# The silu of z as one ScalarE function, two channel blocks to a table load, in place of a tanh and a VectorE product, with small stages moved around it

## The reference, cut to what matters

```python
xz = xn @ W_in
xb, z = jnp.split(xz, 2, axis=-1)
xb = conv_w[:, 0] * xp[:, :-2] + conv_w[:, 1] * xp[:, 1:-1] + conv_w[:, 2] * xp[:, 2:] + conv_b
xb = jax.nn.silu(xb)
dt = jax.nn.softplus(xb @ W_dt + b_dt)
...                      # scan over time: h = exp(dt*A)*h + dt*x*B ; y = sum over states of h*C
y = (y + D_param * xb) * jax.nn.silu(z)
return residual + y @ W_out
```

## Time and profile before

| | |
|---|---|
| median of 3 runs | 2643.23 us (2642.23 to 2643.57) |
| the profiled execution's own time | 2637.64 us |
| its span, first to last instruction | 2635.9 us |
| mean granted TensorE clock | 0.949 |
| busy share PE, DVE, POOL, ACT | 87%, 91%, 86%, 56% |
| slot 6, first to next first scan | 153.8 us |

### The profile page before, as it was taken

The page is one execution under the profiler, slowest core; times in us unless marked ns, Lnnn a source line. Parts: engine busy times, 40 slices in busy tenths (PEclk is TensorE's granted clock), DMA queues, the critical chain, the costliest instruction groups (busy, mean ns, idle before and its releaser), DMA issues.

```text
span 2635.9 us, 28145 instructions
## 1 busy us (share of the span) xinstructions
PE 2303.2 (87%) x8814; PEld 1648.3 (63%) x8814; DVE 2385.8 (91%) x2390; ACT 1489.0 (56%) x2825; POOL 2255.9 (86%) x1591
## 2 busy tenths in 40 slices
PE   6356998989989898998989899898989999898799
PEld 2224675756667576666757666575666667576678
DVE  4999999999999999999999999999999999999922
ACT  5656556565655656565565656556565665654320
POOL 2888999998999899899989998999889899988812
PEclk9677999999999999999999999999989999899899
DMA  6998999989999998989999898998989899898911
GB/s 167 256 218 209 216 224 215 235 207 243 214 219 222 210 243 200 248 215 219 222 206 248 192 246 211 224 224 207 249 193 235 209 229 233 200 249 192 233 49 48
DMA packets 312886, 558.72 MB, mean 212 GB/s; under 512 B 46864, under 2 KB 157456, under 8 KB 312736
## 3 DMA queue, kind: packets, MB, share of 16 engines
q0 software_dynamic: 77568, 260.08, 51.2%
q1 hardware_dynamic: 235168, 296.84, 36.9%
HBM read 295.10 MB, written 10.06 MB: 116 GB/s over the span
## 4 chain that ended last, share of the span: by engine, by line
PE 46%; POOL 20%; DVE 13%; issue 9%; ACT 7%; DMA 5%; SPq 0%; POOLq 0%; DVEq 0%
PE wbank L509 17%; PE mbank L521 9%; POOL unit L1361 8%; DVE hbank L765 7%; PE wbank L410 6%; DMA gsum<-unit 4%; PE wbank L451 4%; PE wbank L536 3%; POOL gsum L1375 3%; POOL act L1328 2%; ACT z L939 2%; POOL stat L1249 2%; ACT hbank L1133 2%; PE wbank L435 1%; PE wbank L471 1%
## 5 line engine op out<-in xcount | busy, mean ns | idle before, releaser
L1361 POOL TENSOR_TENSOR unit<-dtx,b_bc 128x1024 f32<-128x1024 f32 x512 | 1417.3, 2790 | 36.5 <-DVE dtx L842 27.9
L765 DVE TENSOR_TENSOR_SCAN hbank<-hbank,unit 128x1024 f32<-128x1024 f32 x512 | 1173.3, 2292 | 50.3 <-ACT hbank L1133 46.6
L1133 ACT ACTIVATE hbank<-dt,a_neg 128x512 f32<-128x512 f32 x1024 | 669.1, 681 | 241.9 <-DVE unit L778 240.0
L1375 POOL DMA_DIRECT2D gsum<-unit x480 | 560.2, 1167 | 73.1 <-DMA gsum<-unit 35.8
L778 DVE TENSOR_TENSOR unit<-hbank,c_bc 128x1024 f32<-128x1024 f32 x480 | 585.4, 1220 | 22.5
L521 PE MATMUL mbank<-down_t,act 128*128 128x256 f32 x2048 | 525.0, 394 | 27.0 <-POOL act L1328 25.9
L509 PE MATMUL wbank<-h_t,up_t 128*128 128x256 f32 x2048 | 509.9, 394 | 37.7 <-DVE xb L636 27.2
L1328 POOL TENSOR_TENSOR act<-act,w_all 128x512 f32<-128x512 f32 x256 | 410.0, 1602 | 142.0 <-DVE act L743 128.2
L509 PE MATMUL wbank<-h_t,gate_t 128*128 128x256 f32 x2048 | 487.3, 381 | 6.3 <-DVE xb L636 5.6
L521 PEld LDWEIGHTS mbank<-down_t,act 128*128 128x128 f32 x2048 | 398.7, 198 | 148.6 <-issue 51.5
L509 PEld LDWEIGHTS wbank<-h_t,up_t 128*128 128x128 f32 x2048 | 397.8, 197 | 141.3 <-DVE xb L636 38.8
(11 more groups left out here) (140 smaller groups left out, 2210.8 us busy)
## 6 DMA issues: line engine op xcount, KB each, us to landing
gsum<-unit POOLq DMA_DIRECT2D x480, 512.0 KB, 7.9
b_bc<-bc_scratch SPq DMA_DIRECT2D x352, 256.0 KB, 7.2
c_bc<-bc_scratch SPq DMA_DIRECT2D x352, 256.0 KB, 7.2
w_all<-w_scratch SPq DMA_DIRECT2D x256, 256.0 KB, 4.9
ht<-in_L_attn_x_dram SPq DMA_DIRECT2D x16, 512.0 KB, 6.1
w_out<-in_L_attn_W_out_dram SPq DMA_DIRECT2D x16, 512.0 KB, 8.0
ht<-in_L_attn_x_dram POOLq DMA_DIRECT2D x16, 512.0 KB, 8.0
out_dram<-xt SPq DMA_DIRECT2D x16, 512.0 KB, 3.1
```

Source lines behind the costliest of these rows:

```text
L765: eng.tensor_tensor_scan(h, h, unit[:, g % RING, :, :].rearrange("p a t -> p (a t)"), 0.0, ALU.mult, ALU.add).then_inc(scanned, 1)
L1133: eng.activation(hbank[g % HB][:, a, :], dt[:, 2 * q + a, :], ACT.Exp, scale=a_neg[:, 2 * q + a, n:n + 1]).then_inc(decayed, 1)
L1361: eng.tensor_tensor(unit[:, g % RING, :, :], dtx[:, 2 * q:2 * q + 2, :], b_bc[:, s:s + 1, :].to_broadcast([P, 2, T]), ALU.mult).then_inc(d ...
L1375: eng.dma_start(gsum[:, 2 * pair + k, :, :], unit[:, g % RING, :, :], accum_op=ALU.add).then_inc(summed[pair][k], 16)
```

## The change

The gates stage is remade. ACT applies Silu to the bank itself, which frees the bank; DVE's four products for each row are gone, and so is the halving of W_in. Two channel blocks are treated together. The waits of both banks come before the first Silu, in the order of the blocks: the table load stands behind the first bank's wait and the second bank's wait is on the first Silu. Only `mix` now waits on DVE for the gates. The table of moments is changed in most of its rows.

```diff
-                    need.wait_ge(z_halved, 1)
                     for k in range(HK):
                         m = eng.matmul(t.bank[:, :], w_in[:, k, (DK + q) * P:(DK + q + 1) * P], xn_t[:, k, :],
...
-            def gates(row):
-                for q in range(DK):
-                    t = work.at["gate", row, q]
-                    need.wait_ge(gate_act, DK * row + q + 1)
-                    eng.scalar_tensor_tensor(out=gz[:, q, :], in0=gz[:, q, :], scalar=1.0, in1=t.bank[:, :],
-                                             op0=ALU.add, op1=ALU.mult).then_inc(t.free, 1)
...
-                    t = work.at["y", row, q]
+                    z, t = work.at["gate", row, q], work.at["y", row, q]
+                    need.wait_ge(z.free, z.after)
                     need.wait_ge(t.full, t.after)
...
             def gates(row):
-                for q in range(DK):
-                    t = work.at["gate", row, q]
-                    need.wait_ge(t.full, t.after)
-                    if row:
-                        p = work.at["proj", row - 1, 1]
-                        need.wait_ge(p.full, p.after)
-                    eng.activation(gz[:, q, :], t.bank[:, :], ACT.Tanh).then_inc(gate_act, 1)
+                if row:
+                    p = work.at["proj", row - 1, 1]
+                    need.wait_ge(p.full, p.after)
+                for pair in range(2):
+                    yield
                     yield
+                    blocks = [(q, work.at["gate", row, q]) for q in (2 * pair, 2 * pair + 1)]
+                    for _, t in blocks:
+                        need.wait_ge(t.full, t.after)
+                    for q, t in blocks:
+                        eng.activation(gz[:, q, :], t.bank[:, :], ACT.Silu).then_inc(t.free, 1)
+                    yield
                     yield
...
-            def scale_w(row):
-                eng.activation(w_in[:, :, INNER:2 * INNER], w_in[:, :, INNER:2 * INNER], ACT.Copy,
-                               scale=0.5).then_inc(z_halved, 1)
...
-                     ("scale_h", slot, 2, 57, 61), ("gates", slot, 9, 34, 42), ("base1", slot, 2, 16, 20),
+                     ("scale_h", slot, 2, 61, 65), ("gates", slot, 9, 36, 43), ("base1", slot, 2, 9, 15),
-                         ("silu_first", coming, 6, 57, 60), ("silu_last", coming, 6, 61, 66),
+                         ("silu_first", coming, 6, 56, 59), ("silu_last", coming, 6, 60, 66),
-            plan = [("mix1", last, 4, 5, 5), ("project", last, 4, 6, 6),
+            plan = [("mix1", last, 4, 3, 5), ("project", last, 4, 6, 6),
```

More of the change, by code:

```diff
@@ L211, in build @@
         consts = sem("consts")
-        z_halved, base_made = sem("z_halved"), [sem(f"base{pair}_made") for pair in range(2)]
+        base_made = [sem(f"base{pair}_made") for pair in range(2)]
         scaled_w, a_exp, c_act, c_dve, mod_act, mod_dve = (
@@ L306, in streams @@
             behind, coming = slot - 1, slot + 1
[L307 to L308 removed]
+            plan = [] if slot else [("chunks", 0, 2 * (len(chunks) - EARLY), 13, 50),
+                                                ("base0", 0, 2, 4, 5)]
             if behind >= 0:
[L310 removed]
+                plan += [("mix1", behind, 4, 6, 14), ("load_gb", behind, 1, 40, 57),
                          ("project", behind, 4, 15, 23), ("stats", behind, 5, 21, 27),
[L312 to L315 removed]
+                         ("turn", behind, 4, 31, 31), ("pick", behind, 5, 32, 34), ("weigh", behind, 2, 34, 36)]
+            plan += [("step_sizes1", slot, 9, 1, 7), ("load_wo", slot, 1, 42, 42), ("load_ga", slot, 1, 36, 45), ("scale_wo", slot, 1, 38, 50),
+                     ("scale_h", slot, 2, 61, 65), ("gates", slot, 9, 36, 43), ("base1", slot, 2, 9, 15),
+                     ("mix0", slot, 4, 80, 95)]
             if coming < NB:
[L317 to L320 removed]
+                plan += [("load_x", coming, 1, 18, 32), ("norms", coming, 12, 31, 45), ("turn_in", coming, 2, 49, 54),
+                         ("silu_first", coming, 6, 56, 59), ("silu_last", coming, 6, 60, 66),
+                         ("rows_bc", coming, 3, 77, 81),
+                         ("step_sizes0", coming, 9, 72, 82), ("base0", coming, 2, 89, 91)]
             return [Steps(stage[name](row), n, first, final) for name, row, n, first, final in plan if name in stage]
@@ L1212, in _ @@
                         "project": project, "stats": stats, "turn": turn, "weigh": weigh,
-                        "chunks": lambda r: turning, "scale_w": scale_w, "base0": lambda r: base(r, 0),
+                        "chunks": lambda r: turning, "base0": lambda r: base(r, 0),
                         "base1": lambda r: base(r, 1)}
```

23 lines of the change are left out of this document (5 added, 18 removed).

## The result

The changed kernel takes 2676.81 us (median of 4 runs, 2670.33 to 2678.88); before, in the same session, 2642.73 (2637.07 to 2643.57). The ratio is 1.0135 [1.0116, 1.0154]: 34 us slower by the medians (36 by the ratio), where 2633.5 was forecast and the range ended at 2658. The profiled executions are further apart: spans 2677.1 and 2635.9, 41.2 us.

The account below looks back on a forecast made before the run. Bound: PE in its gapless stretches, a POOL-ACT chain with DVE beside it in the gates' stretch. 15 x -0.67 = -10.05, first slot -1.35, end +1.7: -9.7 us, 2633.5 us on the median; range 2612 to 2658.

Parts of the forecast that it names:

- What bounds the kernel: PE in gapless stretches (89.4 of 153.8 us); in the gates' stretch a chain between POOL and ACT, DVE beside it.
- The products' removal: Four DVE products a row, 43.3 us in all; only the first on the chain, about 0.6 a row, offset by ACT's lateness.
- DVE's case: Rival: DVE is the bound everywhere, so removing its products gives -43.3 us, 2599.9; chance 0.05.
- The loads: Gates' stretch: four added table loads and the moved gate, 5.72 us a row, fit into ACT's 5.85 us idle.
- the drain: Rival: each switch pauses about one more load at four switches, some 5 us a row, giving 2737; chance 0.01.
- the rival of the uncovered loads: Exponentials behind the second load pair come late, the scan at 1038.68 starts 1.7 later: +17.2 us, 2660.4; chance 0.20.
- the sign that I had named for it: ACT's wait before the second norm's scaling vanishes and DVE waits for exponentials by over 1.5 us twice a row.
- The convolution: At the second block, DVE's 0.67 us wait for ACT's tanh goes: 15 x -0.67 = -10.05 us.
- The rest of the moves: turn_in, base1, mix0, step_sizes0, rows_bc, base0 and SP's loads: counted at nothing, off the chain or set by PE's pass count.
- First slot: The first slot is DVE's; the four products there may give 0 to 2.7 us, taken as -1.35.
- The end: After the last scan, PE waits longer for the sums' transfer, one experts' product earlier: +1.7 us, bounds 0 and 2.5.

Follow-up runs that it names:

- the run without loads: The changed kernel with the gates' function Tanh instead of Silu, so 64 table loads fewer, all else the same: 2643.98 us, ratio 1.0014.
- the moves alone: The new table of moments with the gates of before (tanh on ACT, product on DVE), no added table load: 2649.84 us, ratio 1.0040.

## Why the prediction was wrong, step by step

**What bounds the kernel: right.** PE in its gapless stretches and a chain between POOL and ACT in the gates' stretch, with DVE beside it. The products' removal changed the time by -0.1% [-0.3%, +0.1%] in the old table, with the functions in pairs, so DVE's case was rightly held small. The chain was told too short: in slot 6 it returns to PE from 1006.84 to 1013.15 (router, down product, gates' product). That lies ahead of the gates' stretch, and no term of the sum used it. DVE's busy time fell by 32.4 us on the page, where I had said about 43. By the groups it is 43.3; but the page counts overlapping moments once, and an instruction starts about 0.1 us before the end of the one ahead of it (0.69 from 1042.97, the next from 1043.57), so 64 products fewer take less off the page than their own times sum to. The waits are not the reason: without loads the page has 2353.6, as with them.

**The loads, first failed step.** "It fits by 0.1 us, if ACT can use every idle moment. ... I take the norms' chain as unchanged". The price of a load was right to the digit (1283 ns), a Silu takes 595 ns, and the drain didn't come. What failed is the sum over the whole stretch of 21.30 us. It mixes idle time that lies on two sides of a fixed point: the second norm's sums, which POOL releases. Ahead of them there was room, and the first pair cost little. Behind them, up to the scaling, before's rows show the 2.33 us ahead of L939 and 0.53 ahead of the squares, some 2.9 us. Before, all four tanhs stood ahead of the sums; now the second pair's 1.09 us stand behind them too, which leaves 1.8 (the run without loads shows 1.83). The second pair's loads need 2.57 and found 0.97. Measured: 1.76 us a row in slot 6, 1.9 as the mean of 13 slots (154.70 to 156.56, the run without loads 154.70 too). That is the rival of the uncovered loads: its mechanism, its place (the exponentials behind the second load pair, scan at 80.5 in the slot, now at 83.5) and its size, 1.7 a row, were right, and so was its condition. One detail was off: the exponentials right behind the load feed the scan before that one (1054.80, which waits 0.43 for them). I gave it 0.20. Its 2660.4 is 16 us short, for the 10 us of gain that it too took for the convolution, and for the first slot and the end. Of the sign that I had named for it, ACT's wait before the second norm's scaling did vanish (none at 1054.63); DVE's long waits were for the experts' tanh (2.21 and 1.07), not twice 1.5 us for exponentials.

**The convolution, second failed step.** "The DVE work up to the second block's end is the same; the 0.67 goes. What is late next is DVE's own work." The wait went, and the two units there got 0.44 us shorter instead of 0.67, while the rest of the slot got longer by more. Taken as -10.05 us; measured alone +11 (0.43% [0.28%, 0.59%]). I had asked only what is late next on DVE, in this stretch. PE waits for the same product through the ring of banks; its waits moved by a block (1.32 and 1.95 became 0.22, 1.64 and 1.27) but did not grow in sum. So the step that failed is to count DVE's 0.67 as time won; what costs the 11 us stays open.

**The rest of the moves, at nothing.** Wrong too: with before's gates the moves without the convolution cost 0.25% [0.13%, 0.37%], 7 us, and I had taken "the count of passes, not their place" as the rule for PE's stretches. It holds only as long as no bank, tanh or transfer is late in them: in slot 6 PE was busy for 52.46 of 52.50 us there and now is for 51.01 of 53.00. Of these 2 us 1.27 are the convolution's; the rest is ahead of down products, which wait about 0.5 us once or twice a row. Which of the moves does it no run shows.

**First slot.** -1.35 taken, +4.8 measured (134.7 to 139.5). Without loads it is 136.2, so most is the loads': ahead of the scans between 100 and 130 us DVE waits 10.9 us for exponentials, 6.6 without loads. The longest two are

```profile
116.84 2.30 DVE L754 TENSOR_TENSOR_SCAN hbank<-hbank,unit 128x1024 f32<-128x1024 f32 x1 [4.66 <-ACT hbank L1121]
129.45 2.30 DVE L754 TENSOR_TENSOR_SCAN hbank<-hbank,unit 128x1024 f32<-128x1024 f32 x1 [4.92 <-ACT hbank L1121]
```

**The end.** +1.7 taken with 2.5 as the bound, +5.2 measured (139.0 to 144.2), the moves alone 144.3. The first of the sums' waits grew from 1.34 to 1.73 (by 0.4, where I had said 1.73), so the term's own mechanism is small. The clock is the larger part, and the sum had nothing for it:

```profile
2538.69 1.10 PE L534 MATMUL wbank<-gsum,ident 128*128 128x512 f32 x2 [1.73 <-DMA gsum<-unit]
2541.07 2.08 PE L534 MATMUL wbank<-gsum,ident 128*128 128x512 f32 x2 [1.29 <-DMA gsum<-unit]
2542.94 3.62 PE L507 MATMUL wbank<-h_t,up_t 128*128 128x256 f32 x8
```

From 2541.0 to 2546.4, behind idle times of 1.73 and 1.29 us, the granted clock is 0.50, the lower level; at the same sums before (from 2505.2, behind 1.34 and 1.29) it is 1.00. The experts' product takes 3.62 us for 1.89, and the eight passes of the sums 5.53 for 3.94: with the longer wait 3.7 us. With the end's stages put back the clock stays up there, and 1.6 of the 5.2 us stay. PE is busy for 132.84 us in the stretch and was for 128.82, with 5 instructions more in it.

**The sum again,** with the traces' sizes: before the first slot +1.3, first slot +4.8, slot 1 +1.2, 13 middle slots 13 x 1.86 = +24.2, the last slot +4.4, the end +5.2: 41.1, the spans' 41.2. Of the middle slots' 1.86 us none is left without the loads; the last slot's 4.4 are all still there.

**What a switch costs.** The Trainium skill, "ScalarE: Activation LUTs", asks in its Rules for kernel authors to do all of one set before switching, and its section What ACT_TABLE_LOAD costs puts a switch at about 2.66 us. The direction was right here, the size not: 64 loads cost 25 to 44 us in four pairs of runs (32, 44, 25, and 41 behind the squares), at most 0.7 us each, and they stood in the rows at 1.28 us with 0.02 us beside them and no drain.

**Open.** Why the move of the convolution costs time though its waits did not grow; which of the moves makes PE's stretches longer; where the last slot's 4.4 us and the end's remaining 1.6 are.

## What to carry to other kernels

Idle time covers new work only if it lies between the same two fixed points as the work: before adding the idle time of a stretch, cut the stretch wherever another engine releases the one that is to take the work, and sum each part alone. The longest wait that a new instruction causes is no measure of its price; follow it to the next point at which two engines meet, and see whether the other one was later anyway. And grouping functions to save table loads holds their PSUM banks longer: with three banks in the ring that was dearer here than the loads (62 loads saved, 88 us lost).

## What the runs showed of the hardware that I had not expected

The tanh behind a Silu needs no load of its own: at 1051.48 the experts' tanh follows the second pair and the load stands only ahead of the exponentials (1052.10), while behind a softplus a load stands ahead of the tanh (14 such loads). And a load can wait for a bank: of ACT's groups in after, the 32 loads to Silu have 11.1 us of idle time before them, for PE's products. There the stage waits for two banks, and the load stands behind the first wait. The 63 loads to softplus have only 1.1 us before them, while the softpluses themselves wait 38.4 us for PE: there the load ran ahead of the wait.

```profile
L997 ACT ACT_TABLE_LOAD x63 | 80.8, 1283 | 1.1
...
L1025 ACT ACT_TABLE_LOAD x32 | 41.1, 1283 | 11.1 <-PE wbank L433 10.6
```
